# Attention stage of a decoder layer: the matrix engine's loop over two chunks instead of four, the exponential's table loaded before the loop, the accumulator copied before the last add

## The chip, the cores and the metric

The kernel runs on one core of a Trainium2 chip. The core has a matrix engine (TensorE, PE in the profile, with its weight loads as PEld), VectorE (DVE), ScalarE (ACT), GpSimd (POOL), a queue engine for DMAs (SyncE, SP) and 16 DMA engines. Each engine runs its own instruction stream; they wait for one another on semaphores. The metric is the device time of one execution in microseconds (us), median of several runs.

## What is computed

Inputs are two sequences of 2048 tokens with 512 features (4096 tokens in all), and a context of 77 rows per sequence. In fp32 the layer is, cut to what matters:

```
# self-attention, 16 heads of 32
qkv = x @ w_qkv.T ; q, k, v = split(qkv)
attn = softmax(q k^T * 32**-0.5)          # per head, 2048 x 2048
x = layernorm(x + (attn v) @ w_out.T + b_out)
# cross-attention, full width, keys = values = ctx
x = layernorm(x + softmax(x ctx^T / sqrt(32)) ctx @ W_out.T)
# feed-forward with fake quantisation of activations and weights
h = quant(silu(gate(quant(x))) * up(quant(x)))
x = layernorm(x + h @ quant(w_down).T)
```

The change touches the first block alone, between the projection of q, k, v and the product with `w_out`.

## The kernel before, in words

`decoder` calls the stages one after the other: `project` (q, k, v to DRAM), `attend` (the softmax and its product with v), `true_max` and `attend_exact` (a second attention that is skipped by a branch unless the numbers leave a safe range), `mix` (output projection, layer norm, cross-attention), `ffn_up` and `ffn_down`. Each stage is a block of five instruction streams, one per engine, written out by hand with semaphore waits; there is no scheduler, so the order in the code is the order on the engine.

`attend` walks over 8 pairs of (group of 4 heads, sequence). That is its outer loop, `Fori(0, ITERS)` with `ITERS = 8`, on every engine, and one pass is called a turn here. A turn has `CPB = 4` chunks of 512 queries, and a chunk has `KB = 16` blocks of 128 keys. All of a turn is written out straight in the loop's body: 64 blocks.

For one block, TensorE's `score` (L814 to L835) makes the scores of 4 heads in 12 matmuls, three terms for each head, since q and k are each held in two parts. The first head's scores go to the PSUM tile `score_first`, of which there is one, the other three heads' to `score_others`, of which there are two. ScalarE takes the exponentials in two instructions, L695 for `score_first` and L696 for `score_others`, into `probs` (or `probs_joined` for blocks 8 to 11 of a chunk). `values` (L854 to L864) multiplies the probabilities with v into `mixed_ps`, 4 matmuls in the code and 8 in the trace, as fp32 takes two passes. TensorE runs `AHEAD = 2` blocks ahead with its scores, and the score of the next block waits until L695 has emptied `score_first`.

The softmax's denominators come from VectorE and GpSimd. VectorE adds the probabilities of 12 of the 16 blocks elementwise into `dve_sum` (L777, 11 adds a chunk); GpSimd's DMA queue adds `probs_joined` 1 to 0 and 3 to 2 (L807, an accumulating DMA). When a chunk is over, TensorE's `sums` (L837 to L852) multiplies these three tiles with ones into `mixed_ps`, in three parts numbered 0, 1 and 2: part 0 waits until VectorE has copied the chunk's result out of `mixed_ps` (`gather`, L704 to L710), parts 0 and 1 wait for the joining DMAs, and part 2 waits for the last add. Then VectorE's `finish` (L712 to L739) transposes the sums out of `mixed_ps` (L718, which signals `sums_read`), inverts and multiplies. The next chunk's first `values` waits for `sums_read`.

The order within a chunk on TensorE is set by the table `VALUES_AT` and by where `sums` stands:

```
VALUES_AT = [[], [], [0], [1, 2], [3], [4, 5]] + [[k] for k in range(6, KB)]
...
for step, blocks in enumerate(VALUES_AT):
    score(it, c * KB + step + AHEAD)
    for at in ((0,), (1, 2))[step] if step < 2 else ():
        sums(it, c, at)
    for k in blocks:
        values(it, c, k)
```

So step 0 is a score and part 0 of the sums, step 1 a score and parts 1 and 2, step 2 a score and block 0's `values`, and from step 6 on each step is one score and one `values`. The last `values` of a chunk comes after the second score of the next. SyncE loads the next turn's keys and values in four pieces during the fourth chunk, and queries chunk by chunk.

Of the kernel before, what the change touches and what calls it, by code (L numbers as in the profile page):

```python
# [5 lines left out]
F32 = mybir.dt.float32  # L6
# [4 lines left out]
ACT = mybir.ActivationFunctionType  # L11
AX = mybir.AxisListType

P = 128
# [8 lines left out]
CPB = SEQ // CH  # L23
KB = SEQ // P
# [520 lines left out]
def attend(nc, io, scr, keep):  # L545
    ITERS = GROUPS * BATCH
    BLOCKS = CPB * KB
# [18 lines left out]
    with ExitStack() as ctx:  # L566
# [11 lines left out]

        w_raw = probs[W_SLOT].rearrange("p (k e) -> p k e", e=D)
        dve_sum = [sb(f"dve_sum{u}", [P, HPG * CH], F32) for u in range(2)]  # L580
        mixed = sb("mixed", [P, CH], F32)

        turned = sb("sums_turned", [P, COLS, HD], F32)
# [32 lines left out]
        with nc.Block() as block:  # L616
# [59 lines left out]
            @block.scalar  # L676
            def _(act):
                act.sem_inc(probs_done, EXPS)
                with act.Fori(0, ITERS) as it:
                    for c in range(CPB):  # L680
                        act.wait_ge(shift_done, it * CPB + c + 1)
                        for k in range(KB):
                            n = c * KB + k
                            if n == W_SLOT:

                                act.wait_ge(w_lo_done, 1)

                            if k in JOINED:
                                act.wait_ge(sums_done, it * CPB + c + 2)
                            elif ADDED.index(k) >= P_RING:  # L690
                                act.wait_ge(dve_added, (it * CPB + c + 1) * ADDS + max(ADDED.index(k) - P_RING, 1))
                            else:
                                act.wait_ge(dve_added, (it * CPB + c) * ADDS + ADDED.index(k) + P_RING)
                            act.wait_ge(scores_done, 1 + it * BLOCKS + n + 1)
                            nc.scalar.activation(block_probs(k)[:, 0:CH], score_first[:], ACT.Exp, bias=shift[:, c:c + 1], scale=SCALE).then_inc(probs_done, 1)  # L695
                            nc.scalar.activation(block_probs(k)[:, CH:HPG * CH], score_others[n % 2][:], ACT.Exp, bias=shift[:, c:c + 1],  # L696
                                                 scale=SCALE).then_inc(probs_done, 1)

                act.wait_ge(probs_done, (ITERS + 1) * EXPS)
                act.sem_inc(probs_done, 1)  # L700

            @block.vector
            def _(v):
# [51 lines left out]
                nc.vector.tensor_copy(keep.w_parts[:, 0], w_raw).then_inc(w_hi_done, 1)  # L755
                v.wait_ge(w_hi_done, 1)
                nc.vector.tensor_tensor(keep.w_parts[:, 1], w_raw, keep.w_parts[:, 0].bitcast(F32), ALU.subtract).then_inc(w_lo_done, 1)
                with v.Fori(0, ITERS) as it:
                    for c in range(CPB):
                        total = dve_sum[c % 2]  # L760
                        gather(it, c)
                        for a in range(ADDS):
                            k = ADDED[a + 1]
                            n = c * KB + k
                            if a == 1:

                                take_shift(it if c == 0 else it + 1, (c + CPB - 1) % CPB)
                                finish(it, c)
                            v.wait_ge(probs_done, (it + 1) * EXPS + (n + 1) * 2)
                            if a == 0:  # L770

                                v.wait_ge(sums_done, 1 + it * CPB + c)
                                first = block_probs(ADDED[0])
                            else:
                                v.wait_ge(dve_added, (it * CPB + c + 1) * ADDS + a)
                                first = total
                            nc.vector.tensor_tensor(total[:], first[:], block_probs(k)[:], ALU.add).then_inc(dve_added, 1)  # L777
                gather(ITERS, 0)
                finish(ITERS, 0)

                v.wait_ge(extremes_done, 2 + 2 * (ITERS * CPB + 1))
# [29 lines left out]

            @block.tensor
            def _(pe):
                def score(it, n):  # L814

                    if n >= BLOCKS:
                        it, n = it + 1, n - BLOCKS
                    c, k = n // KB, n % KB
                    if k % KPP == 0 and c == 0:
                        pe.wait_ge(kv_in[k // KPP], (it + 1) * KV_UP)  # L820
                    if k == 0:
                        pe.wait_ge(q_in[c % 2], it * (16 * CPB // 2) + 16 * (c // 2 + 1))


                    if n == 0:
                        pe.wait_ge(probs_done, it * EXPS + (BLOCKS - 1) * 2 + 1)
                    else:
                        pe.wait_ge(probs_done, (it + 1) * EXPS + (n - 1) * 2 + 1)
                    for t, (a, b) in enumerate(TERMS):
                        for h in range(HPG):  # L830
                            rows = slice(h * HD, (h + 1) * HD)
                            out = score_first[:] if h == 0 else score_others[n % 2][:, (h - 1) * CH:h * CH]
                            last = nc.tensor.matmul(out, k_parts[rows, a, k * P:(k + 1) * P], q_parts[c % 2][rows, b, :],  # L833
                                                    start=t == 0, stop=t == len(TERMS) - 1)
                    last.then_inc(scores_done, 1)  # L835

                def sums(it, c, at):  # L837

                    f = it * CPB + c
                    if at == 0:  # L840
                        pe.wait_ge(mixed_copied, f + 1)
                        pe.wait_ge(filled, 2)
                    if at < 2:
                        pe.wait_ge(joined, 2 * f + at + 1)
                    else:
                        pe.wait_ge(dve_added, (f + 1) * ADDS)
                    part = (probs_joined[0], probs_joined[2], dve_sum[(c + 1) % 2])[at]
                    for j in range(HPG):
                        last = nc.tensor.matmul(mixed_ps[j * HD:(j + 1) * HD, :], keep.ones[:, 0:HD], part[:, j * CH:(j + 1) * CH],  # L849
                                                start=at == 0, stop=at == 2)  # L850
                    if at == 2:
                        last.then_inc(sums_done, 1)  # L852

                def values(it, c, k):  # L854

                    n = c * KB + k
                    pe.wait_ge(probs_done, (it + 1) * EXPS + (n + 1) * 2)
                    if k == 0:

                        pe.wait_ge(sums_read, 1 + it * CPB + c + 1)  # L860
                    for j in range(HPG):
                        last = nc.tensor.matmul(mixed_ps[j * HD:(j + 1) * HD, :], v_group[:, k, j * HD:(j + 1) * HD],  # L862
                                                block_probs(k)[:, j * CH:(j + 1) * CH], start=k == 0, stop=k == KB - 1)
                    last.then_inc(mixed_done, 1)  # L864

                pe.sem_inc(scores_done, 1)
                pe.sem_inc(sums_done, 1)
                for n in range(AHEAD):
                    score(0, n)

                pe.sem_inc(mixed_done, BLOCKS - 1)
                pe.wait_ge(dve_added, ADDS)
                for j in range(HPG):
                    last = nc.tensor.matmul(mixed_ps[j * HD:(j + 1) * HD, :], keep.ones[:, 0:HD], dve_sum[1][:, j * CH:(j + 1) * CH],
                                            start=True, stop=True)
                last.then_inc(mixed_done, 1)
                with pe.Fori(0, ITERS) as it:
                    for c in range(CPB):
                        for step, blocks in enumerate(VALUES_AT):
                            score(it, c * KB + step + AHEAD)  # L880
                            for at in ((0,), (1, 2))[step] if step < 2 else ():
                                sums(it, c, at)
                            for k in blocks:
                                values(it, c, k)
                for at in range(3):
                    sums(ITERS, 0, at)

                pe.wait_ge(col_done, 2)
                for side in range(2):
                    last = nc.tensor.matmul(mixed_ps[0:1, side * P:(side + 1) * P], extremes_col[:, side:side + 1], keep.ident[:],  # L890
                                            start=True, stop=True)
                last.then_inc(row_done, 1)
# [1207 lines left out]
```

## Time and profile before

| | us |
|---|---|
| median of 3 runs | 2004.15 (2004.0 to 2008.56) |
| the profiled execution, its own time | 2009.11 |
| its span, first to last instruction | 2007.0 |
| TensorE busy | 1830.6 (91%) |
| VectorE busy | 1463.2 (73%) |
| ScalarE busy | 1459.6 (73%) |
| GpSimd busy | 161.3 (8%) |

The attention stage runs from about 313 us to 1476 us of the span, more than half of it; projection comes before, and mixing and feed-forward behind. Busy times of an instruction include its pipeline, so that instructions in a row overlap by a tenth of a microsecond, and four matmuls that work on four 32-row strips of the array run at once and count once each. In the windows below stand the stretch, its length, the busy time and instructions of PE, PEld, DVE, ACT and POOL, TensorE's granted clock (1 is its full speed), the DMA share and GB/s. In the waits, who waited for whom, the total in us, how many times and the longest. In the timelines, the first number is the start in us from the start of the span, the second the length of the merged group.

### The profile page before, as it was taken

The page shows a single profiled execution, that of the slowest core. Times are in us where ns is not written, and L with a number is a line of the kernel's source. Part 1 is how long each engine was busy: PE and PEld are TensorE (multiplying, and loading weights), DVE is VectorE, ACT ScalarE, POOL GpSimd, SP SyncE. Part 2 cuts the span into 40 slices and gives each one's busy share as a digit, 9 for nine tenths or more (in the row PEclk, how much of TensorE's full clock was granted, in tenths as well). Part 3 has the DMA queues.
Part 4 walks back from the last instruction along what each step waited for, and adds up shares of the span by engine and source line. Part 5 has one row for each costly group of instructions (what it writes and reads, how often), then busy time and mean ns, then how long its engine had stood idle before and what let it go on. Part 6 is the DMA issues. An engine that isn't in the chain of part 4 may idle for free. (4 is left out here: it accounts for less than half of the span.)

```text
span 2007.0 us, 38852 instructions
## 1 busy us (share of the span) xinstructions
PE 1830.6 (91%) x14516; PEld 850.7 (42%) x14516; DVE 1463.2 (73%) x1579; ACT 1459.6 (73%) x1578; POOL 161.3 (8%) x131
## 2 busy tenths in 40 slices
PE   8999997998998999989989989989949998699786
PEld 6777772332332323323323323323316775344332
DVE  5434436887887987878878878878844776688787
ACT  4443436998998998989989989989924564555465
POOL 0000001000000000000000000000012220000164
PEclk9999997999999999999999999999979997799898
DMA  8656545445354363363553554355356340124174
GB/s 290 222 193 217 213 178 163 96 117 132 80 135 108 75 158 96 85 158 74 106 138 76 115 137 93 88 138 107 89 152 216 134 146 0 58 115 172 58 291 165
DMA packets 111650, 270.15 MB, mean 135 GB/s; under 512 B 7956, under 2 KB 26516, under 8 KB 101780
## 3 DMA queue, kind: packets, MB, share of 16 engines
q1 hardware_dynamic: 98324, 193.05, 26.7%
q0 software_dynamic: 9216, 67.11, 18.0%
q10 hardware_dynamic: 3968, 7.86, 1.0%
q8 instruction: 118, 1.93, 0.4%
q14 instruction: 24, 0.20, 0.0%
HBM read 115.95 MB, written 84.93 MB: 100 GB/s over the span
## 5 line engine op out<-in xcount | busy, mean ns | idle before, releaser
L777 DVE TENSOR_TENSOR dve_sum<-dve_sum,probs 128x2048 f32<-128x2048 f32 x320 | 733.2, 2291 | 81.4 <-ACT probs L696 72.6
L696 ACT ACTIVATE probs<-score_others,shift_now 128x1536 f32<-128x1536 f32 x384 | 613.4, 1597 | 0.0
L833 PE MATMUL score_first<-q_parts,k_parts 32*128 32x512 f32 x1542 | 502.0, 431 | 60.0 <-issue 30.1
L833 PE MATMUL score_others<-q_parts,k_parts 32*128 32x512 f32 x4626 | 507.1, 432 | 0.0
L833 PEld LDWEIGHTS score_first<-q_parts,k_parts 32*128 32x128 f32 x1542 | 249.2, 186 | 534.1 <-ACT probs L695 259.0
L862 PE MATMUL mixed_ps<-probs,v_group 128*32 128x512 f32 x3072 | 395.9, 602 | 0.0
L695 ACT ACTIVATE probs<-score_first,shift_now 128x512 f32<-128x512 f32 x384 | 283.0, 737 | 90.5 <-PE score_others L833 88.4
L833 PEld LDWEIGHTS score_others<-q_parts,k_parts 32*128 32x128 f32 x4626 | 256.9, 186 | 1.4
L696 ACT ACTIVATE probs_joined<-score_others,shift_now 128x1536 f32<-128x1536 f32 x128 | 199.9, 1562 | 0.0
L807 POOL DMA_DIRECT2D probs_joined<-probs_joined x64 | 55.2, 863 | 1100.0 <-PE mixed_ps L862 1069.7
L862 PE MATMUL mixed_ps<-probs_joined,v_group 128*32 128x512 f32 x1024 | 136.4, 605 | 0.0
L862 PEld LDWEIGHTS mixed_ps<-probs,v_group 128*32 128x32 f32 x3072 | 67.0, 108 | 155.7 <-issue 101.1
L1505 PE MATMUL mix_y_ps<-w_out_parts,mix_o_in 128*128 128x512 f32 x384 | 98.2, 410 | 22.6 <-DMA mix_o_in<-o_scratch 22.6
L253 ACT ACTIVATE squares<-proj_ps 128x512 bf16<-128x512 f32 x64 | 38.2, 597 | 101.1 <-PE proj_ps L411 101.1
L411 PE MATMUL proj_ps<-x_hi,qkv_hi 128*128 128x512 f32 x256 | 101.7, 397 | 9.1 <-DVE qkv_lo L312 9.1
L323 DVE TENSOR_TENSOR parts<-proj_ps,parts 128x512 fp32r<-128x512 f32 x64 | 44.0, 690 | 90.1 <-ACT parts L257 90.1
L2021 PE MATMUL down_y_ps<-down_t,down_ints 128*128 128x512 bf16 x352 | 84.3, 403 | 21.1 <-DVE down_ints L1930 21.1
L1694 ACT ACTIVATE up_gated<-up_gate_ps,up_gate_scale 128x512 f32<-128x512 f32 x88 | 59.5, 686 | 59.9 <-PE up_gate_ps L1777 36.7
L695 ACT ACTIVATE probs_joined<-score_first,shift_now 128x512 f32<-128x512 f32 x128 | 89.5, 699 | 16.7 <-PE score_others L833 16.7
L411 PE MATMUL proj_ps<-x_lo,qkv_hi 128*128 128x512 f32 x256 | 100.6, 393 | 0.0
L411 PE MATMUL proj_ps<-x_hi,qkv_lo 128*128 128x512 f32 x256 | 100.5, 393 | 0.0
L718 DVE STREAM_TRANSPOSE sums_turned<-mixed_ps 128x512 f32<-128x512 f32 x33 | 23.7, 717 | 98.7 <-PE mixed_ps L849 98.7
(205 smaller groups left out, 2268.6 us busy)
## 6 DMA issues: line engine op xcount, KB each, us to landing
probs_joined<-probs_joined POOLq DMA_DIRECT2D x64, 1024.0 KB, 8.9
k_parts<-k_scratch SPq DMA_DIRECT2D x36, 512.0 KB, 3.9
q_parts<-q_scratch SPq DMA_DIRECT2D x33, 512.0 KB, 8.2
o_scratch<-out_parts SPq DMA_DIRECT2D x33, 512.0 KB, 2.8
h_scratch<-h SPq DMA_DIRECT2D x6, 2816.0 KB, 8.1
h<-h_scratch SPq DMA_DIRECT2D x6, 2816.0 KB, 10.7
k_scratch<-parts SPq DMA_DIRECT2D x32, 512.0 KB, 3.4
q_scratch<-parts SPq DMA_DIRECT2D x32, 512.0 KB, 2.7
```

The costliest lines, as they stand in the source:

```text
L253: nc.scalar.activation(squares[:, m, :], bank[:], ACT.Square).then_inc(squared, 1)
L323: nc.vector.tensor_tensor(parts[m % RING][:, 1, :], out_ps[m % BANKS][:], parts[m % RING][:, 0, :].bitcast(F32), ALU.subtract).then_inc(pa ...
L411: last = nc.tensor.matmul(bank[:], lhs, rhs, start=t == 0, stop=t == len(terms) - 1)
L695: nc.scalar.activation(block_probs(k)[:, 0:CH], score_first[:], ACT.Exp, bias=shift[:, c:c + 1], scale=SCALE).then_inc(probs_done, 1)
L696: nc.scalar.activation(block_probs(k)[:, CH:HPG * CH], score_others[n % 2][:], ACT.Exp, bias=shift[:, c:c + 1], scale=SCALE).then_inc(prob ...
L777: nc.vector.tensor_tensor(total[:], first[:], block_probs(k)[:], ALU.add).then_inc(dve_added, 1)
L807: nc.gpsimd.dma_start(probs_joined[2 * i][:], probs_joined[2 * i + 1][:], accum_op=ALU.add).then_inc(dma_joined[i], 16)
L833: last = nc.tensor.matmul(out, k_parts[rows, a, k * P:(k + 1) * P], q_parts[c % 2][rows, b, :], start=t == 0, stop=t == len(TERMS) - 1)
L862: last = nc.tensor.matmul(mixed_ps[j * HD:(j + 1) * HD, :], v_group[:, k, j * HD:(j + 1) * HD], block_probs(k)[:, j * CH:(j + 1) * CH], st ...
L1505: last = nc.tensor.matmul(y_ps[t % 2][:], o_in[u][:, k, a, t * P:(t + 1) * P], (w_hi, w_lo)[b][:, k, :], start=m == 0, stop=m == len(terms ...
L1694: nc.scalar.activation(gated[t % 2][:], gate_ps[t % BANKS][:], ACT.Silu, scale=gate_scale[:, t:t + 1]).then_inc(gate_out, 1)
L2021: last = nc.tensor.matmul(y_ps[u][t][:], ints[u][:, r, t * P:(t + 1) * P], keep.down_t[:, r, :], start=r == 0, stop=r == IT - 1)
```

## The change

Three edits, all in `attend`.

1. TensorE's loop runs 16 times over `PAIR = 2` chunks, where it ran 8 times over 4. `score`, `sums` and `values` count in these turns; the waits reach the same values of the same semaphores. The other engines keep their loops of four chunks.
2. ScalarE takes one exponential of a 128x1 tile before its loop, so that the compiler loads the exponentials' table there.
3. VectorE's `gather` (the copy out of `mixed_ps`) stands before the last of a chunk's 11 adds, where it stood before the next chunk's first. The first `gather` moves ahead of the loop.

```diff
@@ scalar
                 act.sem_inc(probs_done, EXPS)
+                nc.scalar.activation(first_exp[:], keep.shift[:, 0:1], ACT.Exp)
                 with act.Fori(0, ITERS) as it:
@@ vector
+                gather(0, 0)
                 with v.Fori(0, ITERS) as it:
                     for c in range(CPB):
                         total = dve_sum[c % 2]
-                        gather(it, c)
                         for a in range(ADDS):
...
                                 finish(it, c)
+                            if a == ADDS - 1:
+                                gather(it, c + 1)
                             v.wait_ge(probs_done, (it + 1) * EXPS + (n + 1) * 2)
...
-                gather(ITERS, 0)
                 finish(ITERS, 0)
@@ tensor
+                PAIR = 2
+                TURNS = ITERS * CPB // PAIR
+                TURN_BLOCKS = PAIR * KB
...
-                        pe.wait_ge(kv_in[k // KPP], (it + 1) * KV_UP)
+                        pe.wait_ge(kv_in[k // KPP], (turn // (CPB // PAIR) + 1) * KV_UP)
                     if k == 0:
-                        pe.wait_ge(q_in[c % 2], it * (16 * CPB // 2) + 16 * (c // 2 + 1))
+                        pe.wait_ge(q_in[c], 16 * (turn + 1))
...
-                with pe.Fori(0, ITERS) as it:
-                    for c in range(CPB):
+                with pe.Fori(0, TURNS) as turn:
+                    for c in range(PAIR):
                         for step, blocks in enumerate(VALUES_AT):
-                            score(it, c * KB + step + AHEAD)
+                            score(turn, c * KB + step + AHEAD)
```

How the streams differ is seen in the instruction listings. First TensorE (PE), the end of the loop in the kernel before; a branch goes back to the loop's start, and the rows between the loop's first and this branch are 612.

```order
L833 MATMUL score_first<-q_parts0,k_parts 128x512
L833 MATMUL score_others1<-q_parts0,k_parts 128x512 x3
L857 REGISTER_ALU
L862 MATMUL mixed_ps<-probs5,v_group 32x512 x4
L877 REGISTER_ALU
L877 COMPARE_AND_BRANCH
L849 MATMUL mixed_ps<-probs_joined0,ones 32x512 x4
```

The same engine and place in the changed kernel.

```order
L840 MATMUL score_first<-q_parts0,k_parts 128x512
L840 MATMUL score_others1<-q_parts0,k_parts 128x512 x3
L863 REGISTER_ALU
L868 MATMUL mixed_ps<-probs5,v_group 32x512 x4
L883 REGISTER_ALU
L883 COMPARE_AND_BRANCH
L856 MATMUL mixed_ps<-probs_joined0,ones 32x512 x4
```

The work around the branch is the same; the branch now closes 309 rows, and it stands behind chunks 1 and 3 of what the other engines call a turn, so that the seam between chunks 1 and 2, straight code before, has a branch too. The loop starts at the same row of the listing in both.

ScalarE (ACT) at the start of its loop, before.

```order
L676 UNCONDITIONAL_BRANCH [waits barrier_Pool_Activation_PE_DVE_SP_release]
L679 UNCONDITIONAL_BRANCH
L679 ISA
L693 ISA [waits shift_done]
L694 ISA [waits dve_added]
L695 ACT_TABLE_LOAD
L695 ACTIVATE probs<-score_first,shift_now 128x512 [waits scores_done]
```

And now.

```order
L677 UNCONDITIONAL_BRANCH [waits barrier_Pool_Activation_PE_DVE_SP_release]
L681 ACT_TABLE_LOAD
L681 ACTIVATE first_exp<-shift 128x1
L682 UNCONDITIONAL_BRANCH
L682 ISA
L696 ISA [waits shift_done]
L697 ISA [waits dve_added]
L698 ACTIVATE probs<-score_first,shift_now 128x512 [waits scores_done]
```

The table load has left the loop's body, in which it stood behind the loop's first row, and no other is in the loop.

VectorE (DVE) from the last two adds of chunk 0 to the transpose in chunk 1, before.

```order
L777 TENSOR_TENSOR dve_sum<-dve_sum,probs 128x2048 [waits dve_added]
L769 REGISTER_ALU
L775 REGISTER_ALU [waits probs_done]
L777 TENSOR_TENSOR dve_sum<-dve_sum,probs 128x2048 [waits dve_added]
L707 REGISTER_ALU
L710 COPY mixed<-mixed_ps 128x512 [waits normal_done,mixed_done]
L769 REGISTER_ALU
L777 TENSOR_TENSOR dve_sum<-probs 128x2048 [waits sums_done,probs_done]
L743 ISA
L743 TENSOR_SCALAR shift_now<-shift 128x1
L716 REGISTER_ALU
L718 STREAM_TRANSPOSE sums_turned<-mixed_ps 128x512 [waits inverse_turned_back,sums_done]
```

And now.

```order
L783 TENSOR_TENSOR dve_sum<-dve_sum,probs 128x2048 [waits dve_added]
L710 REGISTER_ALU
L713 COPY mixed<-mixed_ps 128x512 [waits normal_done,mixed_done]
L775 REGISTER_ALU
L781 REGISTER_ALU [waits probs_done]
L783 TENSOR_TENSOR dve_sum<-dve_sum,probs 128x2048 [waits dve_added]
L775 REGISTER_ALU
L783 TENSOR_TENSOR dve_sum<-probs 128x2048 [waits sums_done,probs_done]
L746 ISA
L746 TENSOR_SCALAR shift_now<-shift 128x1
L719 REGISTER_ALU
L721 STREAM_TRANSPOSE sums_turned<-mixed_ps 128x512 [waits inverse_turned_back,sums_done]
```

The copy, with its wait for `mixed_done` (the chunk's last `values` on TensorE), changed places with the chunk's last add; both adds and the transpose behind it keep their order.

## Rows read from the trace of the kernel before

**Rows 1.** Waits from 315 to 1478 us: TensorE's; total, times, longest.
```profile
PE score_first L833 <- issue: 30.1, 7, 4.5
PE mixed_ps L849 <- DVE mixed L710: 14.1, 26, 1.5
```
**Rows 2.** Timeline of ScalarE: each shown exponential is a chunk's first; last row, last turn.
```profile
456.62 1.28 ACT L695 ACT_TABLE_LOAD   x1
457.92 0.69 ACT L695 ACTIVATE probs<-score_first,shift_now 128x512 f32<-128x512 f32 x1
...
497.25 0.80 ACT L695 ACTIVATE probs<-score_first,shift_now 128x512 f32<-128x512 f32 x1
...
566.01 0.80 ACT L695 ACTIVATE probs<-score_first,shift_now 128x512 f32<-128x512 f32 x1
...
601.92 0.69 ACT L695 ACTIVATE probs<-score_first,shift_now 128x512 f32<-128x512 f32 x1
...
1325.61 0.69 ACT L695 ACTIVATE probs<-score_first,shift_now 128x512 f32<-128x512 f32 x1
```
**Rows 3.** Timeline of TensorE where one turn ends and the next begins.
```profile
459.56 1.07 PE L862 MATMUL mixed_ps<-probs,v_group 128*32 128x512 f32 x8
464.79 0.53 PE L833 MATMUL score_first<-q_parts,k_parts 32*128 32x512 f32 x1 [4.17 <-issue]
...
465.12 0.63 PE L833 MATMUL score_first<-q_parts,k_parts 32*128 32x512 f32 x1
```
**Rows 4.** Windows, busy by engine, clock, DMA: projection turn; behind a seam; attention turn.
```profile
152.10:224.00 71.90, 71.90 (x340) 56.57 (x340) 30.89 (x55) 29.97 (x47) 0.00 (x0) 1.00 0.58 207
...
464.70:468.20 3.50, 3.41 (x24) 1.07 (x28) 0.00 (x0) 1.95 (x2) 0.00 (x0) 0.56 0.43 153
...
464.60:608.60 144.00, 135.75 (x1376) 45.43 (x1376) 119.22 (x88) 131.86 (x129) 6.88 (x8) 0.99 0.47 111
```
**Rows 5.** DMA queues, page; then the only one from 60 to 310; then from 465 to 603.
```profile
q8 instruction: 118, 1.93, 0.4%
...
q1 hardware_dynamic: 25796, 50.77, 56.5%
...
q8 instruction: 12, 0.20, 0.6%
```
**Rows 6.** Timeline of VectorE from a chunk's last adds into the next chunk.
```profile
491.57 9.27 DVE L777 TENSOR_TENSOR dve_sum<-dve_sum,probs 128x2048 f32<-128x2048 f32 x4 [2.21 <-ACT probs L696]
500.76 0.68 DVE L710 COPY mixed<-mixed_ps 128x512 f32<-128x512 f32 x1
501.53 2.29 DVE L777 TENSOR_TENSOR dve_sum<-probs 128x2048 f32<-128x2048 f32 x1
503.74 0.15 DVE L743 TENSOR_SCALAR shift_now<-shift 128x1 f32 x1
505.46 0.72 DVE L718 STREAM_TRANSPOSE sums_turned<-mixed_ps 128x512 f32<-128x512 f32 x1 [1.58 <-PE mixed_ps L849]
```
**Rows 7.** Timeline of TensorE at the same seam, its weight load at 506.23 behind it.
```profile
499.01 1.06 PE L862 MATMUL mixed_ps<-probs,v_group 128*32 128x512 f32 x8
...
501.58 1.07 PE L849 MATMUL mixed_ps<-probs_joined,ones 128*32 128x512 f32 x8 [0.48 <-DVE mixed L710]
...
504.35 1.04 PE L849 MATMUL mixed_ps<-dve_sum,ones 128*32 128x512 f32 x8
...
506.24 1.06 PE L862 MATMUL mixed_ps<-probs,v_group 128*32 128x512 f32 x8
...
506.23 0.16 PEld L862 LDWEIGHTS mixed_ps<-probs,v_group 128*32 128x32 f32 x8 [0.38 <-DVE sums_turned L718]
```
**Rows 8.** VectorE's copy at a turn's end; a joining DMA; landing of all 64.
```profile
460.78 0.69 DVE L710 COPY mixed<-mixed_ps 128x512 f32<-128x512 f32 x1 [0.82 <-PE mixed_ps L862]
...
492.64 0.86 POOL L807 DMA_DIRECT2D probs_joined<-probs_joined  x1 [3.14 <-PE mixed_ps L862]
...
DMA to landing us min/median/max: 7.0/8.9/11.3
```

More of the change, by code:

```diff
@@ L580, in attend @@
         dve_sum = [sb(f"dve_sum{u}", [P, HPG * CH], F32) for u in range(2)]
+        first_exp = sb("first_exp", [P, 1], F32)
         mixed = sb("mixed", [P, CH], F32)
@@ L813, in _, with score @@
             def _(pe):
-                def score(it, n):
-                    if n >= BLOCKS:
-                        it, n = it + 1, n - BLOCKS
+                PAIR = 2
+                TURNS = ITERS * CPB // PAIR
+                TURN_BLOCKS = PAIR * KB
+                def score(turn, n):
+                    if n >= TURN_BLOCKS:
+                        turn, n = turn + 1, n - TURN_BLOCKS
                     c, k = n // KB, n % KB
                     if k % KPP == 0 and c == 0:
-                        pe.wait_ge(kv_in[k // KPP], (it + 1) * KV_UP)
+                        pe.wait_ge(kv_in[k // KPP], (turn // (CPB // PAIR) + 1) * KV_UP)
                     if k == 0:
-                        pe.wait_ge(q_in[c % 2], it * (16 * CPB // 2) + 16 * (c // 2 + 1))
[L825 to L828, printed above, removed]
+                        pe.wait_ge(q_in[c], 16 * (turn + 1))
+                    pe.wait_ge(probs_done, EXPS + turn * (2 * TURN_BLOCKS) + (n - 1) * 2 + 1)
                     for t, (a, b) in enumerate(TERMS):
@@ L832, in score, with sums @@
                             out = score_first[:] if h == 0 else score_others[n % 2][:, (h - 1) * CH:h * CH]
-                            last = nc.tensor.matmul(out, k_parts[rows, a, k * P:(k + 1) * P], q_parts[c % 2][rows, b, :],
+                            last = nc.tensor.matmul(out, k_parts[rows, a, k * P:(k + 1) * P], q_parts[c][rows, b, :],
                                                     start=t == 0, stop=t == len(TERMS) - 1)
                     last.then_inc(scores_done, 1)
-                def sums(it, c, at):
-                    f = it * CPB + c
+                def sums(turn, c, at):
+                    f = turn * PAIR + c
                     if at == 0:
@@ L852, in sums, with values @@
                         last.then_inc(sums_done, 1)
-                def values(it, c, k):
-                    n = c * KB + k
-                    pe.wait_ge(probs_done, (it + 1) * EXPS + (n + 1) * 2)
+                def values(turn, c, k):
+                    pe.wait_ge(probs_done, EXPS + turn * (2 * TURN_BLOCKS) + (c * KB + k + 1) * 2)
                     if k == 0:
-                        pe.wait_ge(sums_read, 1 + it * CPB + c + 1)
+                        pe.wait_ge(sums_read, 1 + turn * PAIR + c + 1)
                     for j in range(HPG):
@@ L876, in _ @@
                 last.then_inc(mixed_done, 1)
-                with pe.Fori(0, ITERS) as it:
-                    for c in range(CPB):
+                with pe.Fori(0, TURNS) as turn:
+                    for c in range(PAIR):
                         for step, blocks in enumerate(VALUES_AT):
-                            score(it, c * KB + step + AHEAD)
+                            score(turn, c * KB + step + AHEAD)
                             for at in ((0,), (1, 2))[step] if step < 2 else ():
-                                sums(it, c, at)
+                                sums(turn, c, at)
                             for k in blocks:
-                                values(it, c, k)
+                                values(turn, c, k)
                 for at in range(3):
-                    sums(ITERS, 0, at)
+                    sums(TURNS, 0, at)
                 pe.wait_ge(col_done, 2)
```

## The prediction

> **What bounds the kernel now.** I began with the waits of TensorE in the attention stage, since it is busy almost throughout: 7 waits put down to "issue", 30.1 us together, so 4.3 each, and 26 short ones for VectorE's copy, 14.1 us together [rows 1]. Seven is the number of times that TensorE's loop goes back.
>
> The size of all this is best read on ScalarE, whose first exponential of each chunk gives the pace [rows 2]. Two chunks in the middle of a turn take 566.01 - 497.25 = 68.76 us, 34.38 each. Sixteen blocks make 2.15 us a block, and both engines set it in parts: from step 6 on ScalarE is never without work, and in the first steps of a chunk, where the sums and double `values` stand, it is TensorE that has more to do. So there are hardly any reserves within a chunk, and a pause at its start is lost. Six turns take 1325.61 - 457.92 = 867.69, 144.6 each, where four chunks of 34.38 are 137.5: 7.1 us of each turn are lost at its seam. The fourth chunk, up to 601.92, is 35.91 long, 1.53 more than a plain one; that is the table load of 1.28 and what it breaks up. The rest, 7.1 - 1.5 = 5.6 us on the mean, is in the first chunk.
>
> TensorE's timeline shows those 5.6 us [rows 3]. The turn's last `values` begin at 459.56, 1.1 us long; the next score comes 4.17 us after their end, at 464.79, and its passes then take 0.63 us where 0.39 is usual: over the 3.5 us behind the seam the granted clock is 0.56 of full speed, so mostly the lower level of 1.2 GHz, after an idle time, and over the turn it is 0.99 [rows 4].
>
> Why does the branch cost that? One queue carries instructions, in packets of 16 KB: 118 in the whole span, and 12 of them while TensorE goes through one turn of attention. From 60 to 310 us there is none, only the data queue, though the projection's loop goes back three times there [rows 5]. That loop has 340 matmuls and 340 weight loads a turn and its TensorE is busy for 71.90 of 71.90 us across the seam. Attention's has 1376 and 1376 [rows 4]. So a body of 680 stays in the engine's instruction memory and its branch is free, and one of 2752 is fetched again each turn, its head only after the branch is taken.
>
> **TensorE's loop of two chunks.** The body is 688 matmuls and 688 weight loads, 1376 and some register work. If it stays in the memory, the 7 pauses and their slow clock go, and the 8 new seams cost nothing that is seen, as in the projection: 7 x 5.6 = 39 us. If it doesn't stay, there are 15 pauses. The trace bounds it by 680, which stays, and 2752, which doesn't. In packets, at 2752 / 12 = 229 matmuls and loads in one, the projection's loop covers 3, attention's 12, the new body 6, and each wants the next one ahead. With the one ahead, 4 packets stay and 13 do not; the new body asks for 7. I take "stays", since 7 is nearer to 4, and since the free loop shows no trace of a limit: no fetch and no idle time in any of its turns.
>
> The Trainium skill speaks of this and on both sides (Runtime: NRT & Kernel Launch, section Instruction fetch mechanics). It gives TensorE's instruction memory as 128 KiB or 2048 instructions, by which the new body fits and the old doesn't; it also says that a taken branch whose target lies outside a window of two pages of 256 instructions has to fetch, by which all 15 branches would pause and the time be that of the first rival below. Of the latter rule the trace doesn't hold for the projection's loop, 680 instructions with no fetch and no idle time.
>
> **The table load.** It leaves the loop: 7 x 1.53 = 10.7 us. The load ahead of the loop is put before a wait for VectorE's first scores' shift and the first scores themselves, so it is hidden there as the first turn's was; uncovered it would cost 1.3 us once.
>
> Together the two edits take 7 x 7.1 = 49.7 us.
>
> **The copy before the last add.** At a plain seam TensorE waits 0.48 us for the copy before part 0 of the sums [rows 7]; 26 such waits are the 14.1 us [rows 1]. The copy started at 500.76, right behind four adds [rows 6], while the chunk's last `values` had begun at 499.01. At a turn's end, where the copy had to wait for TensorE, it began 460.78 - 459.56 = 1.22 us after these started [rows 3, 8]. So it can now begin at 500.23 and part 0 at about 501.10.
>
> The price is that VectorE stands still for it, from 498.55 to 500.23, with an add ready. Queued behind are the last add, the next chunk's first add, the shift and the transpose, for whose end TensorE's next `values` wait. An add is followed by the next instruction after 2.21 us (501.53 to 503.74), 0.08 before its end, and the copy by the same overlap after 0.60. So: copy 500.23, last add 500.83, first add 503.04, shift 505.25, transpose about 505.36, done 506.08. It was done at 506.18, and the `values` behind it were loaded 0.05 later [rows 6, 7]: the 1.58 us in which VectorE had waited for the sums are used up, and of 0.48 us about 0.1 is left. TensorE now waits before block 0's `values` in place of before the sums. From there to block 8 TensorE sets the pace, so this difference stays: 32 x 0.1 = 3 us. The bounds are 0.48 a chunk, 15 us, if VectorE should be earlier than I reckon, and a loss of 0.2 a chunk, 6 us, if its instructions follow one another as dependent adds do, (9.27 - 2.29) / 3 = 2.33 apart. I take 3, as it is built on the same instructions in their rows.
>
> Two waits are near. Part 2 of the sums wants the last add: done at 503.12, wanted at 504.35 - 0.48 = 503.87, 0.75 to spare. Part 1 wants the joining DMA, issued at 492.64 and landed 8.9 us later on the median and 11.3 at most [rows 8]; part 1 stands about one product, 0.9 us, ahead of part 2, so at 502.97. The slowest landing is 1.0 us late for that, of which VectorE's lateness hides 0.4. At the old turns' ends, where four loads of keys share the queues, the 5.6 us pause had hidden it too. I put 2 us on this for the stage.
>
> **The sum.** 49.7 + 3 - 2 = 51 us. The profiled execution took 2009.11 and would take 1958; the median of the runs stands 0.25% lower, 2004.15, and goes to 1953.
>
> **The rivals.**
>
> *The body doesn't stay* (slower). Any way by which the pause belongs to the branch and not to the body's length ends here: 15 pauses for 7. 8 x 5.6 = 44.8 more, less 10.7 for the table and 3 for the copy: +31, 2035 us. It decides from the number of packets the memory holds: 7 needed, at least 4 and fewer than 13 seen. For it speaks that no loop in the trace lies between 680 and 2752; against it, that the free one has no trace of a pause at all.
>
> *The seams lose what the copy gains.* With no pauses, VectorE and the joins run without the slack that a turn's end gave. If the transpose or the join comes 0.5 us late in each of 32 chunks, that is 16 us in place of the gain of 1: about 1970. For it speaks that the reckoning above has VectorE at its limit; against it, that the lateness must exceed the 0.75 and 0.4 us that are spare.
>
> *The copy's wait goes wholly.* If VectorE's transpose keeps up, 0.48 x 31 = 15 us more in place of 1: 1939. Against it stands the 2.29 us add that is now between copy and transpose.
>
> *The table load stays in the loop.* The listing shows none in it, and the rest of the sum would stand: 1964.
>
> **Chances.** Forecast 0.65, body doesn't stay 0.11, seams lose 0.12, wait goes wholly 0.09, table or a part of the pause stays 0.03. A measurement of this kernel can tell about 0.3%, 6 us, from no change. Faster by more than that 0.87, within it 0.02, slower 0.11. The range takes in all but the body that doesn't stay: 1938 to 1973.
>
> **What would show it.** Right: instruction packets fall from 118 to about 30, TensorE's "issue" waits are gone, the granted clock is at full speed through attention, every chunk is about 34.3 us apart on ScalarE, and TensorE's wait for the copy is replaced by short ones in front of block 0's `values`. Wrong: 15 waits of 4 us and a half clock behind each, at every second chunk; or chunks of 34.8 and more with the waits named after the transpose or GpSimd's queue.

## The result, and the profile after

The changed kernel takes 1950.0 us, median of 4 runs (1946.98 to 1951.69), where the kernel before takes 2006.4 (2004.0 to 2010.06, 4 runs): a ratio of 0.9716, 95% interval 0.9694 to 0.9738. The forecast was 1953, with 1938 to 1973 as its range.

The page of the changed kernel begins so; the third line is the queue that carries instructions, with its packets, MB and share of the DMA engines.

```profile
span 1948.4 us, 38894 instructions
...
PE 1814.7 (93%) x14516; PEld 845.0 (43%) x14516; DVE 1456.9 (75%) x1579; ACT 1448.6 (74%) x1572; POOL 161.3 (8%) x131
...
q8 instruction: 21, 0.34, 0.1%
```

118 instruction packets became 21 [rows 5], and ScalarE has 6 instructions fewer: 7 table loads gone, one small exponential more. TensorE's waits in the attention stage, 315 to 1430 us, all of them, as total, times and longest:

```profile
PE score_first L840 <- DMA v_group<-v_scratch: 11.6, 1, 11.6
PE mixed_ps L896 <- DVE extremes_col L794: 4.9, 1, 4.9
PE mixed_ps L856 <- POOLq L815: 1.6, 2, 1.4
PE mixed_ps L856 <- DVE mixed L713: 1.1, 2, 0.8
PE score_first L840 <- ACT probs L698: 0.8, 1, 0.8
```

The 7 waits of 30.1 us for "issue" and 24 of the 26 for the copy [rows 1] are gone. What is left stands at the stage's start and end. ScalarE's first exponentials of five chunks in a row, over the place where the old turn ended:

```profile
454.18 0.80 ACT L698 ACTIVATE probs<-score_first,shift_now 128x512 f32<-128x512 f32 x1
...
488.34 0.81 ACT L698 ACTIVATE probs<-score_first,shift_now 128x512 f32<-128x512 f32 x1
...
522.47 0.80 ACT L698 ACTIVATE probs<-score_first,shift_now 128x512 f32<-128x512 f32 x1
...
556.60 0.80 ACT L698 ACTIVATE probs<-score_first,shift_now 128x512 f32<-128x512 f32 x1
...
590.70 0.80 ACT L698 ACTIVATE probs<-score_first,shift_now 128x512 f32<-128x512 f32 x1
```

They are 34.1 us apart, each of them; four chunks take 590.70 - 454.18 = 136.5, where they took 144.6 on the mean [rows 2]. Seven times 8.1 us is 57, and the median fell by 56. The windows of two such stretches show full clock throughout, the 1.00 ahead of the DMA share:

```profile
454.00:590.50 136.50, 134.50 (x1380) 44.99 (x1383) 118.40 (x89) 130.19 (x129) 6.88 (x8) 1.00 0.48 115
592.00:728.30 136.30, 134.30 (x1380) 44.87 (x1376) 118.27 (x88) 130.07 (x129) 6.88 (x8) 1.00 0.49 115
```

At the seam of two chunks, VectorE's timeline answers to rows 6, and TensorE's to rows 7:

```profile
482.66 6.94 DVE L783 TENSOR_TENSOR dve_sum<-dve_sum,probs 128x2048 f32<-128x2048 f32 x3 [2.24 <-ACT probs L699]
491.24 0.69 DVE L713 COPY mixed<-mixed_ps 128x512 f32<-128x512 f32 x1 [1.63 <-PE mixed_ps L868]
491.85 2.28 DVE L783 TENSOR_TENSOR dve_sum<-dve_sum,probs 128x2048 f32<-128x2048 f32 x1
494.04 2.28 DVE L783 TENSOR_TENSOR dve_sum<-probs 128x2048 f32<-128x2048 f32 x1
...
496.31 0.70 DVE L721 STREAM_TRANSPOSE sums_turned<-mixed_ps 128x512 f32<-128x512 f32 x1
```
```profile
490.10 1.07 PE L868 MATMUL mixed_ps<-probs,v_group 128*32 128x512 f32 x8
...
492.11 1.07 PE L856 MATMUL mixed_ps<-probs_joined,ones 128*32 128x512 f32 x8
...
497.07 1.06 PE L868 MATMUL mixed_ps<-probs,v_group 128*32 128x512 f32 x8
...
497.07 0.16 PEld L868 LDWEIGHTS mixed_ps<-probs,v_group 128*32 128x32 f32 x8 [0.56 <-DVE sums_turned L721]
```

The sums at 492.11 no longer wait for the copy. The 1.58 us for which the transpose had waited now stand ahead of the copy, as 1.63, and the transpose follows its predecessors with no idle time. From a chunk's last `values` to the next chunk's first it is 497.07 - 490.10 = 6.97 us, and was 506.24 - 499.01 = 7.23: the 0.26 us by which a plain chunk is shorter. The weight load of the first `values` waits for the transpose, the new limit of a seam.

### The profile page after: what moved, and what is told of

It reads as the page before. It is cut to its first block and busy times, and to the rows that moved or that the text cites. A ratio compares the mean times of both kernels' runs of the same rounds, so it can differ in the third digit from the quotient of the medians.

```text
span 1948.4 us, 38894 instructions
## 1 busy us (share of the span) xinstructions
PE 1814.7 (93%) x14516; PEld 845.0 (43%) x14516; DVE 1456.9 (75%) x1579; ACT 1448.6 (74%) x1572; POOL 161.3 (8%) x131
## 5 line engine op out<-in xcount | busy, mean ns | idle before, releaser
L699 ACT ACTIVATE probs<-score_others,shift_now 128x1536 f32<-128x1536 f32 x384 | 622.0, 1620 | 0.0
L840 PE MATMUL score_first<-q_parts,k_parts 32*128 32x512 f32 x1542 | 494.1, 425 | 24.2 <-DMA v_group<-v_scratch 11.6
L840 PE MATMUL score_others<-q_parts,k_parts 32*128 32x512 f32 x4626 | 499.0, 426 | 0.0
L840 PEld LDWEIGHTS score_first<-q_parts,k_parts 32*128 32x128 f32 x1542 | 245.0, 183 | 492.2 <-ACT probs L698 288.0
L698 ACT ACTIVATE probs<-score_first,shift_now 128x512 f32<-128x512 f32 x384 | 291.1, 758 | 43.0 <-PE score_others L840 43.0
L840 PEld LDWEIGHTS score_others<-q_parts,k_parts 32*128 32x128 f32 x4626 | 252.6, 183 | 2.2
L1783 PE MATMUL up_gate_ps<-up_ints_t,gate_up_t 128*128 128x512 bf16 x352 | 92.1, 385 | 1.7 <-ACT up_ints_t L1686 1.7
```

The lines of the kernel that those rows point to most:

```text
L1783: last = nc.tensor.matmul(acc[t % BANKS][:], keep.gate_up_t[:, k, first + t * P:first + (t + 1) * P], ints_t[u][:, k, :], start=k == 0, st ...
```

## Experiments: the three edits apart

**TensorE's loop alone.**

```diff
-                with pe.Fori(0, ITERS) as it:
-                    for c in range(CPB):
+                with pe.Fori(0, TURNS) as turn:
+                    for c in range(PAIR):
```

> The kernel before with TensorE's loop over two chunks and nothing else. Theory (the pause at a seam is the fetch of a body that the instruction memory no longer holds): all pauses of 4.3 us and the slow clock behind them go, 7 x 5.6 = 39 us, so 1967 us, 16-KB instruction packets fall to about 20, the table load's 1.5 us at each of 7 seams stays. Rival (the pause belongs to any branch back and only the three edits together hid it): 15 pauses, about 2050 us.

Measured: 1963.6 us, ratio 0.9783 (0.9767 to 0.9799), 21 instruction packets, no "issue" wait. That is 43.5 us for the loop, more than the 39 expected. ScalarE's first exponentials show why, beside its table loads:

```profile
455.41 1.28 ACT L695 ACT_TABLE_LOAD   x1
456.70 0.69 ACT L695 ACTIVATE probs<-score_first,shift_now 128x512 f32<-128x512 f32 x1
...
490.50 0.81 ACT L695 ACTIVATE probs<-score_first,shift_now 128x512 f32<-128x512 f32 x1
...
524.85 0.80 ACT L695 ACTIVATE probs<-score_first,shift_now 128x512 f32<-128x512 f32 x1
...
593.82 1.28 ACT L695 ACT_TABLE_LOAD   x1
595.12 0.69 ACT L695 ACTIVATE probs<-score_first,shift_now 128x512 f32<-128x512 f32 x1
```

A turn is 138.4 us. Its first chunk, 456.70 to 490.50, takes 33.80, shorter by 0.55 than the plain 34.35 behind it. VectorE got ahead during the table load: its copy there waits for TensorE, and not TensorE for the copy.

```profile
459.58 0.69 DVE L710 COPY mixed<-mixed_ps 128x512 f32<-128x512 f32 x1 [0.82 <-PE mixed_ps L863]
```

The table load makes its own chunk longer by 1.5 us and the next one shorter by 0.55, so it costs 0.95 us a turn when there is no pause. The rival, by which any branch back pauses, is out: there are 15 branches.

**The table load alone.**

```diff
+                nc.scalar.activation(first_exp[:], keep.shift[:, 0:1], ACT.Exp)
                 with act.Fori(0, ITERS) as it:
```

> The kernel before with the exponentials' table loaded ahead of ScalarE's loop and nothing else. Theory (the load delays the exponential that TensorE's last score of the turn waits for, so it adds to the pause): 7 x 1.53 = 10.7 us, 1996 us. Rival (the load lies beside TensorE's pause and is hidden by it): no change, 2006 us, and the first chunk of a turn longer by what the last one loses.

Measured: 2002.3 us, ratio 0.9976 (0.9967 to 0.9986), 4.7 us and so between the two. The fourth chunk lost its 1.5 us, but the pause grew, 7 waits of 37.0 us for 30.1:

```profile
462.15 0.79 PE L836 MATMUL score_first<-q_parts,k_parts 32*128 32x512 f32 x1 [5.52 <-issue]
```

The branch has a record of its own in the trace, beside the rows shown. It took 5.7 to 6.0 us in the kernel before and takes 6.6 to 7.2 here. Why is tried below.

**The copy alone.**

```diff
-                        gather(it, c)
...
+                            if a == ADDS - 1:
+                                gather(it, c + 1)
```

> The kernel before with VectorE's copy ahead of the chunk's last add and nothing else. Theory (the new limit is the transpose, 5.1 us behind the copy, whatever else is changed): 24 to 25 plain chunks gain 0.26 us each as in the changed kernel, 6 us, 2000 us; chunks behind a pause gain nothing. Rival (the prediction's reckoning, 0.1 us a chunk): 3 us, 2004 us. Both below what TensorE waited for the copy, 0.5 us a chunk.

Measured: 2001.3 us, ratio 0.9971 (0.9959 to 0.9982), 5.7 us, which is the theory's 6 more than the prediction's 3, though the interval (3.6 to 8.2 us) all but reaches the latter. The trace decides it: most plain chunks of this run are 34.11 to 34.14 us long, as in the changed kernel, where 34.37 was usual before.

**Loop and table without the copy.**

> The changed kernel without the copy's move (loop over two chunks and table load ahead). Theory: 49.7 us of the gain, 1957 us, every chunk 34.38 us apart, against 34.12 in the changed kernel. Rival (the copy's move pays more than 0.26 us a chunk once seams have no pause, since a late joining DMA then decides): chunks of 34.5 and more, 1962 us.

Measured: 1956.9 us, ratio 0.9759 (0.9742 to 0.9776), 34.37 us between any two chunks but the first two, as the theory has it. The rival, by which late joining DMAs would lengthen the chunks of this run, is out.

The parts add up in this order: the loop 43.5, the table behind it 6.6, the copy behind both 6.9; together 57, against 56.3 for the changed kernel, beside whose runs the kernel before stood 0.7 us lower. The last term compares two sets of four runs each and is good to some us; the chunks of the two traces, 34.37 and 34.12, make it 0.25 x 31 = 7.8.

## Experiments: what makes a branch back dear

The bodies with a free branch and with a dear one lay far apart. To get between, idle instructions were put into the changed kernel's loop, increments of a semaphore for which nobody waits, so many behind each of its 32 steps. The branches stay 15, the work stays the same. Counted between two branches in TensorE's record, the body of the changed kernel is 1457 instructions.

```diff
                             for k in blocks:
                                 values(turn, c, k)
+                            for _ in range(8):
+                                pe.sem_inc(pad, 1)
```

> The changed kernel with 8 semaphore increments, which nobody waits for, behind each of the 32 steps of TensorE's loop: some 256 instructions more in the body, about 1700 in all, 7 packets and the one ahead. Theory (a memory of 8 packets, 2048 instructions): the body still stays, no pause, 1950 us. Rival (the memory holds less than 8): 15 pauses of 6 us, 2040 us. Either way the branches are as many as in the changed kernel.

Measured: 2066.7 us in one run, 130 packets. The body is 1713 instructions. Of the 15 branches 12 took 6.7 to 7.6 us and 3 took 0.22 or 0.23. One pause in TensorE's timeline:

```profile
395.53 0.79 PE L841 MATMUL score_first<-q_parts,k_parts 32*128 32x512 f32 x1 [6.88 <-issue]
```

My theory of 8 packets had forecast no pause, and failed as written. That the body's instructions and not the branch are the cause is shown, since nothing differs from the changed kernel but instructions that do nothing. Each turn that paused fetched 9 packets, and the other three fetched none.

> The same with 16 increments a step: about 1950 instructions, 8 packets and the one ahead. Theory (8 packets, the one ahead among them): the head is overwritten, 15 pauses, 2040 us and some 150 instruction packets. Rival (the pauses need a body longer than 2048 instructions, or a memory of 12 packets): no pause, 1950 us.

Measured: 2432.6 us in one run, 173 packets.

> The same with 24 increments a step: about 2200 instructions, more than 2048. Theory: 15 pauses, 2040 us, the same loop and the same number of branches as the changed kernel, so that only the length of the body can be the cause. Rival (the branch of the old loop was dear for another reason than its length): no pause, 1950 us.

Measured: 3080.0 us in one run, 189 packets. In both all 15 branches pause, for 3.3 to 5.0 us. Their times say nothing about the pause, since so many increments are no longer hidden beside the matmuls and slow each step (and with 24 the granted clock of the whole run fell to 0.83, for 0.97); only the packets and the branches were of use. The 256 instructions a turn between the two runs bring 189 - 173 = 16 packets in 15 turns, so that a packet is about 256 instructions.

The mixed outcome at 1713 was odd. Where TensorE crosses from one packet to the next can be told from the times at which packets are fetched: the loop starts about 70 instructions into a packet, so that a body of 1713 ends close to the end of its seventh, some ten instructions ahead of it. This is an estimate from fetches whose places scatter by 20 instructions and more, and not read from a row. Reading on past the branch, the engine could at times touch the eighth packet, which calls for the ninth, and that one would take the place of the loop's head.

The number of packets fetched in a turn that paused fits this. By the same place the body of the kernel before, 2908 instructions, ends in the middle of its twelfth packet, and it fetched 13 a turn: those it touches and one ahead. The bodies with 8, 16 and 24 increments touch 7, 8 and 9 and end close to an edge, and they fetched 9, 10 and 11: one more. Two runs tell this from a plain limit on the length.

> The changed kernel with 6 idle semaphore increments behind each step of TensorE's loop: 1649 instructions a turn, 64 fewer than the run with 8, in which 12 of 15 branches paused. Theory (the memory holds 8 packets of 256; the longer body ended a few instructions ahead of a packet's end, and reading on fetched a ninth): no branch pauses, about 20 instruction packets, 1955 us. Rival (the memory holds 7 packets with the one ahead, or 1600 instructions): most branches still pause, 2060 us.

Measured: 1948.7 us in one run, 22 packets, no branch longer than 0.24 us. The increments cost nothing.

```diff
+                for _ in range(220):
+                    pe.sem_inc(pad, 1)
                 with pe.Fori(0, TURNS) as turn:
```

> The body of 1713 instructions, with 220 more increments ahead of the loop, which move its start and its end within the packets by 220, so that it ends some 40 instructions ahead of a packet's end and not 6. Theory (whole packets count): no branch pauses, about 20 packets, 1980 us with 11 us for the increments ahead. Rival (the body's length alone counts): 12 to 15 pauses as in the run with the same body, 2075 us.

Measured: 1992.0 us in one run, 23 packets, and all 15 branches 0.21 to 0.24 us. The instruction queue (packets, MB, share) with the body of 1713 instructions at its first place, then shifted:

```profile
q8 instruction: 130, 2.13, 0.5%
```
```profile
q8 instruction: 23, 0.38, 0.1%
```

TensorE's longest waits from 310 to 1460 us in the shifted run:

```profile
PE score_first L841 <- issue: 38.9, 33, 30.8
PE score_first L841 <- DMA v_group<-v_scratch: 9.5, 1, 9.5
```

One of them, 30.8 us, is the row of 220 increments ahead of the loop, dearer than the 11 us expected; the other 32 are a quarter of a microsecond each, no pause among them. The same body of 1713 instructions paused 12 times in 15 where it started 220 instructions earlier. So whole packets of 256 instructions count. The reading that fits all of these runs (those with increments were made once each) is that a body that touches 7 packets, with the one ahead, stays; where it touches or nearly touches an eighth, its head is gone.

The Trainium skill's figure for TensorE (Runtime: NRT & Kernel Launch, section Instruction fetch mechanics), 128 KiB or 2048 instructions in blocks of 16 KiB, is 8 such packets, and the runs agree with it. Its sentence that a branch outside of a window of two pages pauses doesn't hold here: the bodies of 1457 and 1649 instructions touch 6 and 7 and branch back in 0.2 us.

**The pause behind the data.** The kernel with the table load alone, and the next turn's keys and values loaded in 16 columns where 512 or 128 were. It leaves most keys and values out, so that its attention is wrong after the first turn.

```diff
-                                load_kv(ng, nb, piece)
+                                load_kv(ng, nb, piece, 16)
```

> The kernel before with the table load ahead of the loop, and the loads of the next turn's keys and values cut to 16 columns, so that attention after the first turn runs on wrong numbers: a look at the pause alone. Theory (the missed head of the body is fetched behind the data of these loads in the DMA queues; with the table load gone the branch comes 1.5 us earlier and meets more of them, which is why the pause grew from 5.8 to 6.8 us): the branch takes 4 us or less in all 7 seams, and the time falls by 7 x 2.8 = 20 us and more, to 1982 us. Rival (the fetch takes as long by itself): 6 to 7 us as with the full loads, 2002 us.

Measured: 1978.3 us in one run. All 7 branches took 4.6 to 4.7 us, for 6.6 to 7.2 with the full loads. The windows are the first 3 us of a branch each, and the last two numbers are the DMA engines' share and GB/s. First with full loads, then with small ones:

```profile
455.00:458.00 3.00, 1.63 (x20) 0.35 (x12) 2.96 (x3) 3.00 (x3) 0.00 (x0) 1.00 1.10 229
```
```profile
453.20:456.20 3.00, 1.73 (x20) 0.42 (x16) 2.97 (x3) 3.00 (x3) 0.00 (x0) 1.00 0.73 144
```

The packet that holds the loop's head starts to move 4.2 to 4.7 us behind the branch's start with full loads, 3.2 to 3.5 in the kernel before, and 2.2 to 2.4 with small ones; the branch ends 2.3 to 2.5 us after that in all three. So 2 to 2.5 us of the pause was the wait of the head's fetch behind loads of keys and values that fill the DMA engines.

The remainder of 4.6 is more than the 4 or less that I expected, and the run with 16 increments shows why: the DMA engines are still busy with other transfers. There every second branch falls where nothing is loaded, and the next one beside the loads:

```profile
413.00:416.00 3.00, 0.00 (x0) 0.00 (x0) 3.00 (x2) 0.26 (x1) 0.00 (x0) 1.00 0.02 5
511.20:514.20 3.00, 0.00 (x0) 0.00 (x0) 3.00 (x2) 0.27 (x1) 0.00 (x0) 0.70 0.77 244
```

At a DMA share of 0.02 the branches of this run and of that with 24 increments take 3.3 to 4.0 us, beside the loads 4.1 to 5.0.

The time fell by 24 us against the run with the table load alone, and the waits by 37.0 - 21.8 = 15 us. Part of the rest is the clock. Behind three of the seven pauses, now 3.1 us long, the granted clock stays full, where it fell to the lower level behind every pause of the kernel before:

```profile
883.50:887.00 3.50, 2.94 (x36) 1.32 (x40) 1.28 (x2) 1.92 (x2) 0.00 (x0) 1.00 0.50 155
```

In the kernel before, the table load delays the branch: the last load issued ahead of it stands 7.5 us before the branch (451.41 and 458.9), and 6.2 with the table load gone (448.85 and 455.0). The branch then meets more of that load's data and its pause is 1 us longer. This is where most of the gain of that edit goes when it is made alone.

## Experiments: the new limit of a seam

**The whole finish ahead of the first add.**

```diff
-                            if a == 1:
+                            if a == 0:
                                 take_shift(it if c == 0 else it + 1, (c + CPB - 1) % CPB)
                                 finish(it, c)
```

> The changed kernel with VectorE's finish (transpose and the rest) ahead of a chunk's first add, where it stood behind it. Theory (the first values of a chunk wait for the transpose, which waits for two adds behind the copy): the transpose starts when the sums are done, 0.2 us earlier than now, chunks of 33.95 us for 34.12, 1945 us. Rival (VectorE then stands still for 2 us more a chunk, has no reserve left and its adds set the pace): chunks of 34.3 and more, 1956 us.

Measured: 1978.6 us, ratio 0.9853 (0.9834 to 0.9871), 29 us more than the changed kernel; chunks of 34.9. The rival was right on the sign, and the loss was larger than it said. ScalarE's row is that of a chunk's seventh block:

```profile
507.62 0.69 ACT L698 ACTIVATE probs<-score_first,shift_now 128x512 f32<-128x512 f32 x1 [1.62 <-DVE dve_sum L783]
```

That exponential goes into the buffer of the chunk's first block, and the add that frees it had been put behind all of finish, 4.2 us of small instructions. It isn't VectorE's total that decides but when the first add is done.

**The transpose alone ahead of it.**

```diff
+                            if a == 0:
+                                turn_sums(it, c)
                             if a == 1:
                                 take_shift(it if c == 0 else it + 1, (c + CPB - 1) % CPB)
                                 finish(it, c)
```

Here `turn_sums` is the transpose of `mixed_ps` with its two waits, taken out of `finish`.

> The changed kernel with the transpose of the sums alone, not the whole of VectorE's finish, ahead of a chunk's first add. Theory (the first add then ends about 2 us before ScalarE needs its buffer, and the first values of a chunk start 0.15 us earlier): chunks of 33.95 to 34.0 us, 1946 us. Rival (VectorE is now without any reserve, since it stands still for 1.6 us behind the add of block 14 and for 1.9 us ahead of the transpose): chunks of 34.2 or more, 1953 us.

Measured: 1946.1 us, ratio 0.9695 (0.9682 to 0.9708), the best of all; its interval overlaps that of the changed kernel, so the times alone don't settle that it is faster. The traces do for the stage. Below are ScalarE's last exponentials for `score_first` ahead of three chunks: they are 33.94 and, over the seam of a turn, 34.11 us apart, and 33.93 elsewhere, for 34.12.

```profile
419.64 0.78 ACT L698 ACTIVATE probs<-score_first,shift_now 128x512 f32<-128x512 f32 x1
...
453.58 0.78 ACT L698 ACTIVATE probs<-score_first,shift_now 128x512 f32<-128x512 f32 x1
...
487.69 0.79 ACT L698 ACTIVATE probs<-score_first,shift_now 128x512 f32<-128x512 f32 x1
```

VectorE at the seam, where the transpose now waits 1.98 us for the sums and the first add is done before ScalarE asks for its buffer:

```profile
493.18 2.28 DVE L789 TENSOR_TENSOR dve_sum<-dve_sum,probs 128x2048 f32<-128x2048 f32 x1
497.44 0.72 DVE L720 STREAM_TRANSPOSE sums_turned<-mixed_ps 128x512 f32<-128x512 f32 x1 [1.98 <-PE mixed_ps L863]
498.08 2.25 DVE L789 TENSOR_TENSOR dve_sum<-probs 128x2048 f32<-128x2048 f32 x1
```

## Why the prediction was right, point by point

- *The time.* A gain of 51 us was forecast and 56.3 measured. That 1953 lies so near to 1950 is in part luck: the three runs of the kernel before had a median 2.2 us below that of the four.
- *What bounds the kernel.* Right: 7.1 us a turn lost at its seam, with the branch back as the larger cause. The loop alone brought 43.5 us.
- *The body stays.* Right in outcome, and for the reason given: 21 packets for 118 (about 30 forecast), no pause with 15 branches. The 12 packets a turn left out the seam, where one more comes, and the 229 in one left out register work; 13 a turn and 256 in one give the same 6 for the new body. The argument that 7 is nearer to 4 than to 13 was a guess; the runs put the edge right behind 7 touched packets, so the forecast stood closer to the other side than its chance of 0.11 says. 256 more instructions at this place in the packets bring most pauses back.
- *The split of the 49.7 us.* The sum was right, 50.1 measured, as the whole 7.1 us a turn was read from ScalarE's rows and both edits together take it; the terms were mis-sized. The loop brought 43.5 for 39, the table behind it 6.6 for 10.7. I had read the table load as serial, since it makes its own chunk 1.53 us longer; the step that failed is that nothing gives it back. The next chunk's copy wait does, 0.55 us of it, and where the pause is in place the branch takes 1 us more once the table load is gone, so that this edit alone brought 4.7.
- *The copy.* The mechanism was right step by step: copy, last add, first add, transpose, and the first `values` as the new place of the wait. The term was mis-sized, 3 us for the 6.9 measured between the runs without and with it. Of the 0.16 us a chunk that the reckoning lacked, half is the copy's start, 1.14 us behind the last `values` and not the 1.22 read at a turn's end, and most of the rest the chain behind it, 496.31 - 491.24 = 5.07 for 5.13. The bounds of 0.48 and -0.2 a chunk hold; the 0.1 within them was the difference of two chains of 7 us, from rows that vary by some hundredths each, and was taken too exactly.
- *The joining DMAs.* 2 us were set aside and TensorE's matmuls wait 1.6 us for them in all, 1.3 before. No chunk of the trace is more than 0.06 us above 34.12 behind the first, so this term is nothing.
- *The rivals.* "The seams lose what the copy gains" didn't come, but finish_first shows it: with the small instructions at the wrong side of an add, the chunk is 34.9 and the cause is ScalarE's buffer, not the transpose. "The wait goes wholly" would have needed the transpose out of the way; taking it out brought 0.19 of the 0.22 us that were left.

## What to carry to other kernels

Count the packets of 256 instructions that TensorE's loop body touches, its place in them included, and keep them with the one ahead within what the engine holds. A trace shows a body that is too long by the instruction queue's packets and by "issue" waits at even distances. Halving the unrolled body cost nothing here. An edit's price depends on what stands beside it: the same table load was worth 4.7 us with the pause and 6.6 without. Where an instruction is moved past others on one queue, ask for each of those it is put ahead of who needs it next, and move the smallest one that the waiting engine wants.

## What the runs showed of the hardware

- A branch back within the held packets takes 0.21 to 0.25 us and shows no "issue" wait. One to a packet that must be fetched took 3.3 to 4.0 us where the DMA engines were at a share of 0.02, 4.6 at 0.73, and 5.7 to 7.2 where loads filled them.
- With 8 increments the branches that paused took 6.7 to 7.1 us where no keys and values are loaded and 6.9 to 7.6 where they are, at a DMA share of 0.96 and more in both. Two instruction packets come at once behind the branch (at 391.19 and 391.40), and the branch ends 4.0 to 4.2 us after the first of them, for 2.3 to 2.8 in the other runs, where one comes. Whether the second packet is the cause is not shown.
- The same body of 1713 instructions paused in 12 of 15 turns or in none, by 220 instructions more or less ahead of the loop.
- Semaphore increments on TensorE's queue are hidden at 6 a step of 2 us (1948.7 us with them, 1950.0 without), and 220 in a row took 30.8 us, 0.14 each.
